# A graph network's attention phase: exponentials as the stationary operand, gathered rows with a column of ones as the moving one, and one more step of lag

## What is computed

```python
for t in range(N_TYPES):                       # 3
    xw = x @ W[t]
    a_s, a_d = xw @ att_src[t], xw @ att_dst[t]
    e_raw = leaky_relu(a_s[src] + a_d[dst], 0.2)         # where edge_type == t
    m = maximum(segment_max(e_masked, dst), e_self)
    w_edge = where(mask, exp(e_raw - m[dst]), 0)
    denom = segment_sum(w_edge, dst) + w_self
    num = segment_sum(w_edge[:, None] * xw[src], dst) + w_self[:, None] * xw
    out_sum += num / denom[:, None] + bias[t]
```

## Time and profile before

| | us |
|---|---|
| Time, median of 3 runs (lowest to highest) | 4478.28 (4478.07 to 4479.33) |
| The profiled execution: its time, its span | 4478.6, 4476.9 |
| Busy in the span: PE, POOL, DVE, ACT | 3882.1 (87%), 3141.5 (70%), 2398.9 (54%), 1538.2 (34%) |
| First gather of the attention, last addition of it ends | 93.75, 2307.04 |

### The profile page before, as it was taken

One profiled execution on the slowest core, in us unless ns is written; L12 is line 12 of the kernel. 1 busy time (PEld: TensorE's weight loads), 2 busy tenths in 40 slices (PEclk: granted clock), 3 DMA queues, 4 the chain that ended last, 5 costly groups with the idle time before them and its releaser, 6 DMA issues. The chain is left out here.

```text
span 4476.9 us, 58713 instructions
## 1 busy us (share of the span) xinstructions
PE 3882.1 (87%) x16856; PEld 2886.7 (64%) x16857; DVE 2398.9 (54%) x5463; ACT 1538.2 (34%) x4513; POOL 3141.5 (70%) x3275
## 2 busy tenths in 40 slices
PE   7899999999999999999966888888888888898888
PEld 5566666666666666666655666666666666676666
DVE  6777777777777777777755332333333333233333
ACT  4555555555555555555532111111111111111111
POOL 3777767777767777777726777777777777777774
PEclk9555555555555555555557776666666676666667
DMA  2222222222222222222234222222222222222223
GB/s 86 51 54 51 51 50 51 51 51 51 51 50 51 51 51 51 51 50 51 51 78 123 74 72 73 73 73 72 73 73 73 73 73 74 74 73 74 73 74 74
DMA packets 149067, 288.41 MB, mean 64 GB/s; under 512 B 78388, under 2 KB 86249, under 8 KB 144542
## 3 DMA queue, kind: packets, MB, share of 16 engines
q0 software_dynamic: 105472, 222.39, 21.6%
q1 hardware_dynamic: 43570, 65.72, 5.2%
HBM read 278.00 MB, written 9.81 MB: 64 GB/s over the span
## 5 line engine op out<-in xcount | busy, mean ns | idle before, releaser
L54 POOL DMA_INDIRECT ae_xg<-table,ae_idx x1620 | 1545.2, 954 | 632.3 <-issue 536.2
L54 POOL DMA_INDIRECT ce_xg<-table,ce_idx x1620 | 1536.7, 949 | 496.8 <-issue 494.7
L1120 DVE TENSOR_TENSOR ce_ps_f<-ce_ps_f,ce_fb 128x768 f32<-128x768 f32 x270 | 261.0, 967 | 1288.4 <-PE ce_ps_f L1071 1286.4
L1092 PE MATMUL ce_ps_h<-ce_ea,ce_fw 50*128 50x384 f32 x1080 | 628.6, 721 | 335.3 <-DMA ce_ea<-in_edge_attr 334.3
L1051 ACT ACTIVATE ce_hid<-ce_ps_h,ce_fb 128x768 f32<-128x768 f32 x270 | 243.5, 902 | 1788.5 <-PE ce_ps_h L1092 1788.5
L605 PE MATMUL ae_ps_a<-ae_e,ae_xg 128*128 128x96 f32 x3240 | 776.0, 430 | 41.0 <-ACT ae_e L534 21.4
L605 PEld LDWEIGHTS ae_ps_a<-ae_e,ae_xg 128*128 128x128 f32 x3240 | 711.3, 329 | 106.1 <-ACT ae_e L534 64.1
L1071 PEld LDWEIGHTS ce_ps_f<-ce_fw,ce_hid 128*128 128x128 f32 x3240 | 594.6, 280 | 228.9 <-issue 215.9
L1071 PE MATMUL ce_ps_f<-ce_fw,ce_hid 128*128 128x128 f32 x3240 | 664.7, 382 | 0.0
L611 PE MATMUL ae_ps_a<-ae_e,cst 128*1 128x96 f32 x3240 | 602.9, 358 | 0.0
L1092 PEld LDWEIGHTS ce_ps_h<-ce_ea,ce_fw 50*128 50x128 f32 x1080 | 255.8, 262 | 479.0 <-issue 248.8
(11 more groups left out here) (138 smaller groups left out, 3003.5 us busy)
## 6 DMA issues: line engine op xcount, KB each, us to landing
ce_ea<-in_edge_attr SPq DMA_DIRECT2D x90, 450.0 KB
ae_xg<-table,ae_idx POOLq DMA_INDIRECT x1620, 2.6
ce_xg<-table,ce_idx POOLq DMA_INDIRECT x1620, 2.5
fa_inv_den<-rden SPq DMA_DIRECT2D x7, 1344.0 KB, 7.5
table<-pr_rows POOLq DMA_DIRECT2D x7, 462.0 KB, 4.1
pr_x<-in_x SPq DMA_DIRECT2D x7, 448.0 KB, 3.3
fa_x<-in_x SPq DMA_DIRECT2D x7, 448.0 KB, 3.4
table<-fa_hd POOLq DMA_DIRECT2D x7, 448.0 KB, 3.7
```

The costliest lines, as they stand in the source:

```text
L54: eng.indirect_dma_start(out=out, out_offset=None, in_=table[:, :], in_offset=bass.IndirectOffsetOnAxis(ap=idx, axis=0)).then_inc(done, 16)
L1092: last = nc.tensor.matmul(ps_h[:, k * 512:k * 512 + H], fw1[:, :], ea[:, s // LOAD, q:q + H], start=True, stop=True)
L1120: nc.vector.tensor_tensor(filt, filt, fb2[:, :].unsqueeze(1).to_broadcast([P, CH, D]), ALU.add).then_inc(s_bias, 1)
```

## The change

The operands of `sums` change places. The exponentials of a chunk (96 keys) become the weights, and the gathered rows move, now 129 columns wide: the pad of a row becomes a column of ones between the features and the scores, so the sum of exponentials comes out as column 128 of the same product, and `totals` goes away. The result has a key to a partition (96 x 129, in one bank `ps_k`). ScalarE copies it to SBUF (`copy_sums`, into `by_key`), and TensorE turns it back (`back`: a transpose of 96x128 and a product of the last column with the identity) into one bank `ps_a`. `ps_m` gets a second buffer, so `rescales` can run late.

The pieces also move. `sums` of a unit runs one step later (step n+3, in two halves where `totals` stood), with `copy_sums` and `back` in the same step; `scale` is at n+3 and `add_sums` at n+4. A slot of `xg` is freed by the second half of `sums`. On VectorE `subtract` waits for `maxima` and not for `rescales`, and stands behind `add_sums`, `scale` and `leaky`. The number of steps with a full set of pieces stays 270, with four steps to drain the pipeline instead of three.

```diff
-ROW = 132
+ROW = D + 1 + NT
...
-                nc.scalar.copy(rows[:, s, :, D:D + NT], ps_s[:, 8:8 + NT * G].rearrange("p (t k) -> p t k", k=NT)).then_inc(s_as, 1)
+                nc.scalar.copy(rows[:, s, :, D + 1:ROW], ps_s[:, 8:8 + NT * G].rearrange("p (t k) -> p t k", k=NT)).then_inc(s_as, 1)
...
-            nc.vector.memset(rows[:, :, :, D + NT:ROW], 0.0)
+            nc.vector.memset(rows[:, :, :, D:D + 1], 1.0)
...
-        ps_tz, ps_c, ps_m = pb("ps_tz"), pb("ps_c"), pb("ps_m")
-        ps_a = [pb(f"ps_a{b}") for b in range(2)]
+        by_key = sb("by_key", [KEYS, D + 1])
+        ps_tz, ps_c, ps_k, ps_a = (pb("ps_" + k) for k in "tz c k a".split())
+        ps_m = [pb(f"ps_m{b}") for b in range(2)]
...
-        less_max, rescale = ps_m[:, 0:KEYS], ps_m[:, KEYS:2 * KEYS]
+        less_max, rescale = ([ps_m[b][:, k * KEYS:(k + 1) * KEYS] for b in range(2)] for k in range(2))
...
-            gather_units(pool, h, table, xg, ROW, idx, idx_in, gathered, xg_free, pool_turn)
+            gather_units(pool, h, table, xg, ROW, idx, idx_in, gathered, s_sum, pool_turn)
...
-                def rescales(n):
-                    act.wait_ge(s_less, n)
-                    nc.scalar.activation(rescale, rescale, ACT.Exp).then_inc(s_rescale, 1)
+                def rescales(s):
+                    nc.scalar.activation(rescale[s % 2], rescale[s % 2], ACT.Exp).then_inc(s_rescale, 1)
+                def copy_sums(n, fresh):
+                    if not fresh:
+                        act.wait_ge(s_back, n - 1)
+                    act.wait_ge(s_sum, n + XS)
+                    nc.scalar.copy(by_key[:, :], ps_k[0:KEYS, 0:D + 1]).then_inc(s_by_key, 1)
...
-                        lag1, lag2 = not (first and s < 1), not (first and s < 2)
-                        if lag2:
-                            rescales(n - 2)
+                        lag1, lag2, lag3 = (not (first and s < k) for k in (1, 2, 3))
                         if lag1:
                             uppers(n - 1)
+                        elsewhere(s, i * SL + s)
+                        if lag3:
+                            copy_sums(n - 3, first and s == 3)
                         if lag2:
                             exps(n - 2, s - 2)
-                        elsewhere(s, i * SL + s)
                         raw(n, s, first and s == 0)
+                        if lag2:
+                            rescales(s - 2)
...
-            pe.sem_inc(xg_free, XS)
+            pe.sem_inc(s_sum, XS)
...
-                def sums(n, s, fresh):
-                    pe.wait_ge(s_e, n)
-                    if not fresh:
-                        pe.wait_ge(s_den, n - 2)
-                    for c in range(CH):
-                        last = nc.tensor.matmul(ps_a[s % 2][:, 0:KEYS], xg[:, s % XS, c, 0:D], by_chunk[s % 3][:, c, :], start=(c == 0), stop=(c == CH - 1))
-                    last.then_inc(xg_free, 1)
-                def totals(n, s, chunks):
+                def sums(n, s, chunks, fresh):
+                    if 0 in chunks:
+                        pe.wait_ge(s_e, n)
+                        if not fresh:
+                            pe.wait_ge(s_by_key, n - 1)
                     for c in chunks:
-                        last = nc.tensor.matmul(ps_a[s % 2][64:65, KEYS:2 * KEYS], h.ones[:, 0:1], by_chunk[s % 3][:, c, :], start=(c == 0), stop=(c == CH - 1))
+                        last = nc.tensor.matmul(ps_k[0:KEYS, 0:D + 1], by_chunk[s % 3][:, c, :], xg[:, s % XS, c, 0:D + 1], start=(c == 0), stop=(c == CH - 1))
                     if CH - 1 in chunks:
                         last.then_inc(s_sum, 1)
+                def back(n, fresh):
+                    pe.wait_ge(s_by_key, n)
+                    if not fresh:
+                        pe.wait_ge(s_den, n - 1)
+                    nc.tensor.transpose(ps_a[:, 0:KEYS], by_key[:, 0:D], h.ident[0:KEYS, 0:KEYS])
+                    nc.tensor.matmul(ps_a[64:65, KEYS:2 * KEYS], by_key[:, D:D + 1], h.ident[0:KEYS, 0:KEYS], start=True, stop=True).then_inc(s_back, 1)
...
-                def maxima(n):
+                def maxima(n, s):
                     pe.wait_ge(s_rise, n)
-                    nc.tensor.matmul(ps_m[:, 0:2 * KEYS], h.less_row32[0:64, :], rise[:, :, :].rearrange("p a k -> p (a k)"),
+                    nc.tensor.matmul(ps_m[s % 2][:, 0:2 * KEYS], h.less_row32[0:64, :], rise[:, :, :].rearrange("p a k -> p (a k)"),
                                      start=True, stop=True).then_inc(s_less, 1)
...
                         if lag2:
                             highest_row(n - 2)
                         if lag3:
-                            totals(n - 3, s - 3, range(0, CH // 2))
+                            sums(n - 3, s - 3, range(0, CH // 2), first and s == 3)
                         if lag2:
-                            maxima(n - 2)
+                            maxima(n - 2, s - 2)
+                        targets(n, base[s], first and s == 0)
                         if lag3:
-                            totals(n - 3, s - 3, range(CH // 2, CH))
-                        targets(n, base[s], first and s == 0)
-                        if lag2:
-                            sums(n - 2, s - 2, first and s < 4)
+                            sums(n - 3, s - 3, range(CH // 2, CH), False)
+                            back(n - 3, first and s == 3)
...
                 def subtract(n, s):
+                    dve.wait_ge(s_less, n)
+                    nc.vector.tensor_tensor(by_chunk[s % 3], by_chunk[s % 3], less_max[s % 2].unsqueeze(1).to_broadcast([P, CH, KEYS]),
+                                            ALU.add).then_inc(s_sub, 1)
+                def scale(n, s, base, fresh, final):
+                    win = bass.ds(base, W)
                     dve.wait_ge(s_rescale, n)
-                    nc.vector.tensor_tensor(by_chunk[s % 3], by_chunk[s % 3], less_max.unsqueeze(1).to_broadcast([P, CH, KEYS]),
-                                            ALU.add).then_inc(s_sub, 1)
-                def scale(n, base, fresh, final):
-                    win = bass.ds(base, W)
                     if not fresh:
                         dve.wait_ge(s_den, n - 1)
-                    nc.vector.tensor_tensor(acc[:, :, win], acc[:, :, win], kv(rescale), ALU.mult)
-                    last = nc.vector.tensor_tensor(state[64:65, :, win], state[64:65, :, win], kv(ps_m[64:65, KEYS:2 * KEYS]), ALU.mult)
+                    nc.vector.tensor_tensor(acc[:, :, win], acc[:, :, win], kv(rescale[s % 2]), ALU.mult)
+                    last = nc.vector.tensor_tensor(state[64:65, :, win], state[64:65, :, win], kv(rescale[s % 2][64:65, :]), ALU.mult)
                     if final:
                         last.then_inc(s_scaled, 1)
-                def add_sums(n, s, base, final):
-                    b = s % 2
+                def add_sums(n, base, final):
                     win = bass.ds(base, W)
                     if final:
-                        dve.wait_ge(s_scaled, r + 1)
-                    dve.wait_ge(s_sum, n)
-                    nc.vector.tensor_tensor(acc[:, :, win], acc[:, :, win], kv(ps_a[b][:, 0:KEYS]), ALU.add)
-                    nc.vector.tensor_tensor(state[64:65, :, win], state[64:65, :, win], kv(ps_a[b][64:65, KEYS:2 * KEYS]), ALU.add).then_inc(s_den, 1)
+                        dve.wait_ge(s_scaled, 2 * r + final)
+                    dve.wait_ge(s_back, n)
+                    nc.vector.tensor_tensor(acc[:, :, win], acc[:, :, win], kv(ps_a[:, 0:KEYS]), ALU.add)
+                    nc.vector.tensor_tensor(state[64:65, :, win], state[64:65, :, win], kv(ps_a[64:65, KEYS:2 * KEYS]), ALU.add).then_inc(s_den, 1)
                 def step(n, s, i, unit, base, stages, fresh):
-                    look, chain, weigh, merge = (k in stages for k in range(4))
+                    look, chain, weigh, rescaled, merge = (k in stages for k in range(5))
...
                         raise_max(n - 2, base(2))
                     if chain:
                         mask(n - 1, s - 1)
+                    if merge:
+                        add_sums(n - 4, base(4), s - 1 if i is None and s > 1 else 0)
+                    if rescaled:
+                        scale(n - 3, s - 3, base(3), fresh and s == 3, i is None and s > 0)
+                    if chain:
+                        leaky(n - 1, s - 1)
                     if weigh:
                         subtract(n - 2, s - 2)
-                    if merge:
-                        add_sums(n - 3, s - 3, base(3), i is None and s == 2)
-                    if weigh:
-                        scale(n - 2, base(2), fresh and s == 2, i is None and s == 1)
                     if chain:
-                        leaky(n - 1, s - 1)
                         highest(n - 1, s - 1)
```

(28 more changed lines are left out.)

20 lines of the change are left out of this document (11 added, 9 removed).

## The result

The changed kernel takes 4336.18 us in the median (4334.89 to 4337.11, 4 runs) where the kernel before took 4478.17 beside it (4474.89 to 4479.33, 4 runs): a ratio of 0.9684, 95% interval 0.9667 to 0.9701, 142 us less. Forecast were 4342 us, 136 less. The profiled execution took 4336.4 us, its span 4334.8.

The account below looks back on a forecast made before the run. VectorE's order plus three round trips was taken as the bound, not TensorE. Cutting the step from 8.027 to 7.52 us over 269 steps saves 136.4 us of 4478.6, giving 4342 us; range 4324 to 4396.

Parts of the forecast that it names:

- VectorE's loop with the 0.55 us in it: VectorE's operations between successive `highest_key`, 7.86 us, including a 0.55 us wait before `subtract` that the change would remove.
- TensorE's ring: TensorE's order from `highest_key` through `sums`, copy and `back` to `turned`: about 7.43 us, ready 0.05 us before wanted.
- A half of `sums`: Six products on TensorE with 96 weight columns and 129 moving, priced from profile rows at 1.37 us.
- Three loops end together: Attention step: VectorE 7.48, GpSimd 7.49, TensorE about 7.43 us; taken as 7.52; chance of this tie 0.55.
- VectorE's 7.31 us: VectorE's step after the change, 7.86 less 0.55 us, before the 0.167 us surplus; 7.48 with it.
- The turned maximum's return: VectorE's wait from the end of `highest` through TensorE's `turned` to the next `highest_key`: 0.75 us, as before.
- The other piece: VectorE's spacing of `leaky`, `subtract` and `highest`: starts at 3.88, 4.67 and 5.45 us after `highest_key`.
- the turn's end: Where engines load addresses after six steps: 1.0 us a turn, 0.167 us a step, left unchanged.
- GpSimd's floor: Rival, chance 0.10: TensorE streams faster or its clock rises, so gathers alone set the attention step, mean 7.48: 4331 us.
- The 0.03 us added for three loops that disturb one another: Allowance per attention step above the longest loop, for disturbance at the ends of turns, giving 7.52 us.
- The drain: Work after the last `highest_key` in the attention: 10.8 us, against 10.84 before the change.
- the gathers' 7.49: GpSimd's time for a unit's gathers, read where it ran without waiting, units 3 to 26: 7.494 us, unchanged.

Follow-up runs that it names:

- old_vector_order: Changed kernel with `subtract` again straight behind `mask`, waiting for `rescales`, which run first in ScalarE's step: 4468.6 us, ratio 0.9975 to the kernel before.
- old_operands: Changed kernel's order and lag, but features as weights again, `totals` restored, no copy or turn back: 4338.08 us, ratio 0.9690 to the kernel before.
- the run with five gathers: Changed kernel with five of six gathers per attention unit, the sixth chunk held at zero: 4243.0 us, ratio 0.9471 to the kernel before.
- the steps with more copies: Changed kernel with extra ScalarE copies of the sums, on slowed chips: ratios to the kernel before 1.0074 and 1.0143 (one copy), 1.0157 (three).
- old_operands_five_gathers: Changed kernel with features as weights and `totals` again, and five of six gathers: ratios 0.9675 and 0.9689 to the kernel before, on slowed chips.

## Why the prediction was right, and where its reasons were not

*The cause of the gain* was named rightly: VectorE's loop with the 0.55 us in it, not TensorE's 92% of busy time. Put the order back and the gain goes, with TensorE relieved all the same (old_vector_order); keep the order and put the operands back and it stays (old_operands, though with a granted clock of 0.59 where the changed kernel has 0.50). The extra step of lag is in all of these runs, and what it is worth alone isn't shown. The cause has two parts, the wait given up and the place behind `leaky`, which the prediction counted as one edit and the runs priced at 69 and 63 us.

*TensorE's ring* was priced well. Counted from `highest_key` at 0, as in the prediction, the run with five gathers has the first half of `sums` at 0.72 (0.85 forecast), `maxima` at 2.15 (2.22), `targets` at 3.08 (3.16), the second half at 3.75 (3.71), the copy at 5.39 with 0.26 us (5.29, 0.25), `back` at 5.71 (5.63) and `turned` at 6.54 (6.53). TensorE waits 0.35 us for the copy, where the forecast times leave 5.63 - 5.29 = 0.34. A half of `sums` takes 1.43 us to the next start, where 1.37 was worked out from rows. By the gap in the Trainium skill (TensorE: Matmul & The Clock Gate, Back-to-back issue gap) it would have been 0.65, an estimate; the Trainium skill says there that this gap is that of a matmul by itself, with no share for loading weights. The 1.43 us at 1.2 GHz don't bear the estimate out for these float32 products, each with a load of its own.

*The step that failed is "Three loops end together".* The mis-sized term is VectorE's 7.31 us, which is 6.97 to 7.02. Two pieces of it were too long. The turned maximum's return was put at 0.75 "as now"; it takes 0.54, as the first L704 of the earlier trace rows had shown. In the earlier trace rows `sums` (L605, from 1208.77, 2.88 us long) still runs when `turned` starts at 1211.44, so I take the 0.21 us for a queue behind it; in old_operands, where `totals` stands there, the return takes 1.32 us ahead of the L706 at 453.49. Against this, the prediction had read that `sums` fits into the loop beside `leaky` and `highest`. The other piece: `leaky`, `subtract` and `highest` follow one another after 0.68 and 0.66 us, where I had put 0.79 and 0.78. `leaky` itself starts 0.11 us later than forecast, so `highest` ends at 6.48 and not at 6.58. Together the two make about 0.3 us. TensorE's ring ends with the same return and shrinks with it, so these two loops do end nearly together, as the steps with more copies show, but at 6.97. With 0.18 for the turn's end VectorE's loop is 7.15, below the gathers' 7.50, so GpSimd alone sets the step: the mechanism of the rival called GpSimd's floor, which I gave 0.10, though not for the reason that I gave there (neither did the clock rise nor did the products stream faster). The 0.03 us added for three loops that disturb one another weren't there: 7.504 for 7.52, which is 4 us of the 6 by which the forecast missed; the rest lies at the ends and behind the attention. The drain, in which the last steps empty the pipeline, took 10.16 us from the last `highest_key` to the last addition, 10.8 forecast. That the number agreed is in part luck: the gathers' 7.49 was read rightly, and the tie was put only 0.03 us above it.

*What is not settled* is what the swap of operands would be worth in a kernel without the gathers' floor. At 1.2 GHz the old operands make a step of 7.76 us and the new ones one of 6.97; but with the old ones the clock doesn't stay there, and old_operands_five_gathers ran only where pauses disturbed it.

## What to carry to other kernels

Follow the engine whose order closes the loop, not the busiest one, and ask of each wait in it two things: does it need that producer, and could it stand later, behind work that is ready? Here both answers were worth some 65 us each. The rearranged products, the larger part of the edit, added nothing to the time as long as the gathers set the step. When a loop is shortened, look for the next floor in the trace of before, at the place where an engine still ran free: GpSimd's units 3 to 26 gave a time of 4331 us, 5 below the measured one.
